# The folded down rows of an FFN taken through DRAM, with other staging places and another order of the first loads

## The reference

```python
# mixer: a decaying scan over the context, projected, averaged over time, added as one row per batch
x = einsum(kv, W_in) + b_in;  s = K*s + xt (scan);  summary = mean(states @ W_out.T + b_out)
y = Z + summary;  return layernorm(y) * gamma + beta
# FFN: a Hadamard transform ahead of up/gate and one ahead of down
x = fwht(x * SU_ug) / SCALE
x_up, x_gate = x @ W_up.T * (...), x @ W_gate.T * (...)
x = fwht(silu(x_gate) * x_up * SU_dp) / SCALE        # over 2048 columns
x = x @ W_down.T * (Wscale_dp * SCALE)
```

## Time and profile before

| | us |
|---|---|
| median of 3 runs (lowest, highest) | 1591.33 (1587.85, 1596.97) |
| the profiled execution | 1594.04 |
| its span | 1592.0 |
| PE busy | 1426.4 (90%) |
| DVE busy | 1015.2 (64%) |
| ACT busy | 508.8 (32%) |
| POOL busy | 385.4 (24%) |

### The profile page before, as it was taken

How to read it: one execution, slowest core, us unless ns; L and a number is a source line. 1 busy time by engine, 2 the same in 40 slices (tenths; PEclk the granted TensorE clock), 3 DMA queues, 4 the chain that set the end, 5 groups by cost and what they waited for, 6 DMA issues and landing times.

```text
span 1592.0 us, 27268 instructions
## 1 busy us (share of the span) xinstructions
PE 1426.4 (90%) x7616; PEld 770.5 (48%) x7617; DVE 1015.2 (64%) x2461; ACT 508.8 (32%) x922; POOL 385.4 (24%) x315
## 2 busy tenths in 40 slices
PE   5569999999999999888988559997989999999797
PEld 3224444444444444444444236654555666666464
DVE  6738866964874555577775546654556666666465
ACT  1324443443343333322222123322222333333232
POOL 1000000000000000034555534342334433444243
PEclk9789999999999999999999779998999999999899
DMA  9664776765675687646747558887888989899787
GB/s 377 167 229 166 248 238 222 240 223 191 210 243 193 216 273 252 224 147 221 256 190 261 197 174 221 226 197 172 207 216 207 236 234 233 219 221 228 165 146 130
DMA packets 133349, 342.82 MB, mean 215 GB/s; under 512 B 15152, under 2 KB 19760, under 8 KB 126896
## 3 DMA queue, kind: packets, MB, share of 16 engines
q1 hardware_dynamic: 74464, 207.51, 39.4%
q0 software_dynamic: 34928, 87.05, 24.2%
q10 hardware_dynamic: 23904, 47.61, 9.7%
HBM read 190.23 MB, written 147.69 MB: 212 GB/s over the span
## 4 chain that ended last, share of the span: by engine, by line
PE 59%; DMA 16%; DVE 8%; issue 7%; SPq 4%; another core or an unknown queue 3%; ACT 3%; ACTq 1%; POOLq 0%; DVEq 0%
PE PS L1394 16%; PE PS L1392 16%; PE PS L1393 16%; DMA rows_by_expert<-X 6%; DMA BIG<-split_experts 4%; PE PS L1620 3%; DMA split_experts<-HT 2%; PE PS L1647 1%; PE PS L1646 1%; SPq L348 1%; DMA BIG<-in_wdT 1%; PE PS L1355 1%; PE PS L1530 1%; PE PS L1635 1%
## 5 line engine op out<-in xcount | busy, mean ns | idle before, releaser
L557 POOL DMA_INDIRECT out<-BIG,EX x160 | 249.1, 1557 | 412.9 <-issue 206.0
L1392 PE MATMUL PS<-BIG 128*128 x804 | 276.0, 343 | 2.8 <-issue 2.0
L1393 PE MATMUL PS<-BIG 128*128 x804 | 275.9, 343 | 0.0
L1394 PE MATMUL PS<-BIG 128*128 x804 | 275.6, 343 | 0.0
L1392 PE MATMUL PS<-HT,BIG 128*128 128x512 f16 (+1 forms) x512 | 195.0, 381 | 7.1 <-ACT EX L607 2.8
L1393 PE MATMUL PS<-HT,BIG 128*128 128x512 f16 (+1 forms) x512 | 194.8, 380 | 0.0
L1394 PE MATMUL PS<-HT,BIG 128*128 128x512 f16 (+1 forms) x512 | 194.6, 380 | 0.0
L535 POOL DMA_INDIRECT rows_by_expert<-HT,POS x128 | 124.3, 971 | 141.7 <-DVE POS L1211 107.6
L1392 PE MATMUL PS<-BIG,EX 128*128 128x512 f16 (+1 forms) x384 | 146.3, 381 | 6.4 <-DVE EX L1153 5.0
L1393 PE MATMUL PS<-BIG,EX 128*128 128x512 f16 (+1 forms) x384 | 146.2, 381 | 0.0
L1394 PE MATMUL PS<-BIG,EX 128*128 128x512 f16 (+1 forms) x384 | 146.0, 380 | 0.0
(11 more groups left out here) (224 smaller groups left out, 2244.1 us busy)
## 6 DMA issues: line engine op xcount, KB each, us to landing
BIG<-rows_by_expert ACTq DMA_DIRECT2D x166, 280.0 KB
HT<-in_experts SPq DMA_DIRECT2D x64, 640.0 KB, 4.6
BIG<-split_experts SPq DMA_DIRECT2D x32, 1152.0 KB
split_experts<-HT SPq DMA_DIRECT2D x96, 320.0 KB, 2.5
CST<-in_kv SPq DMA_DIRECT2D x64, 256.0 KB, 4.5
split_context<-RT SPq DMA_DIRECT2D x64, 256.0 KB, 4.3
BIG<-split_context SPq DMA_DIRECT2D x8, 2048.0 KB
rows_by_expert<-X SPq DMA_DIRECT2D x32, 280.0 KB
```

Of the source, the lines that this page charges most:

```text
L557: pool.indirect_dma_start(a_out, bass.IndirectOffsetOnAxis(ap=IDY[:, u % V:u % V + 1], axis=0), yt[u % V], None, compute_op=ALU.add).then_ ...
L1392: mm(out, lh, rh, start=first, stop=False)
L1393: mm(out, lh, rl, start=False, stop=False)
L1394: return mm(out, ll, rh, start=False, stop=last_group)
```

## The change

Four things change.

1. **wd1 goes through DRAM.** ACT stores four blocks of wd1 (1 MB) at a time to a new DRAM tensor `d_down`, from its own queue, as soon as they are copied. SP waits for all four stores (`s_wst`, 64) and loads chunks 0 to 3, 4 to 7 and later 8 to 15 in three transfers. The sixteen moves are gone.
2. **Other staging places.** Weights chunk 1 is staged at BIG 8192 (inside wd1) and no longer at X 2048, chunk 2 at BIG 10240, and so on. SP loads chunks 0, 1 and 2, POOL the other five. The load of batch 1's x no longer waits for `s_wul` but for `s_w2p` = 4.
3. **Order of the first loads.** The first of the six context loads goes ahead of x, the second between two loads of W_down, one weights chunk ahead of the fourth context load, and the last two context loads behind the router's weights and the first context piece.
4. **Sums of context spread singly.** `sum_context(n)` is now one of twelve sums. Two stand ahead of batch 0's first layer norm, none ahead of `spread(0)`, four between the splits of the transposed tiles, one ahead of each Hadamard split, two behind the last.

```diff
-        wst = [f32(t, o, (KC, 512)) for t, o in ((HT, 0), (X, 2048), (BIG, 8192), (BIG, 10240),
-                                                 (BIG, 12288), (BIG, 14336), (X, 4096), (X, 6144))]
+        wst = [f32(t, o, (KC, 512)) for t, o in ((HT, 0), (BIG, 8192), (BIG, 10240), (BIG, 12288),
+                                                 (BIG, 14336), (X, 4096), (X, 6144), (X, 4096))]
-            def move_chunk(c):
-                sp.dma_start(wd2_chunk(c), wd1[c * 8:(c + 1) * 8, :, :].rearrange("p b d -> p (b d)"))\
-                    .then_inc(s_rel[min(c // 4, 2)], 16)
-
+            def load_chunks(i):
+                first, count = (0, 4, 8)[i], (4, 4, 8)[i]
+                sp.dma_start(wd2[i], d_down.rearrange("(c p) d -> p c d", p=P)[:, first:first + count, :]).then_inc(s_rel[i], 16)
+
+            load_context(0)
             load_x(0, TT)
...
             load_piece(0)
-            sp.wait_ge(s_w1, FC)
-            for c in range(FC):
-                if c == 8:
-                    sp.wait_ge(s_ttr, KC + 8)
-                    for h in range(2):
-                        sp.dma_start(est[h], a_exp[0:1, :, h * EH:(h + 1) * EH].rearrange("a p w -> p (a w)")).then_inc(s_est[h], 16)
-                move_chunk(c)
+            for h in range(4, 6):
+                load_context(h)
+            sp.wait_ge(s_wst, 16 * 4)
+            for i in range(2):
+                load_chunks(i)
+            for c in range(1, 3):
+                load_weights(c)
+            sp.wait_ge(s_ttr, KC + 4)
+            load_chunks(2)
+            sp.wait_ge(s_ttr, KC + 8)
+            for h in range(2):
+                sp.dma_start(est[h], a_exp[0:1, :, h * EH:(h + 1) * EH].rearrange("a p w -> p (a w)")).then_inc(s_est[h], 16)
             sp.wait_ge(s_w2p, 4)
-            load_weights(1)
-            sp.wait_ge(s_wul, 2)
             load_x(TT, 2 * TT)
...
-            pool.wait_ge(s_rel[2], 16 * 8)
-            for c in range(2, 4):
-                load_weights(c)
-            pool.wait_ge(s_wul, 3)
             pool.wait_ge(s_st, 2)
+            load_weights(3)
+            pool.wait_ge(s_sb, 1)
             load_weights(4)
...
             for i in range(FC):
                 down_rows(i)
+                if i % 4 == 3:
+                    act.wait_ge(s_w1, i + 1)
+                    act.dma_start(d_down.rearrange("(p b) d -> p b d", b=FC)[:, i - 3:i + 1, :], wd1[:, i - 3:i + 1, :])\
+                        .then_inc(s_wst, 16)
...
+            for n in range(2):
+                sum_context(n)
             dve.wait_ge(s_x, 16)
             mixer_ln(0, 0)
...
             inverse_root(0)
-            for h in range(2):
-                sum_context(h)
             dve.wait_ge(s_rows, 80)
             spread(0)
...
             for k in range(KC):
+                if k != 2:
+                    sum_context(2 + min(k, 2))
+                else:
+                    ffn_weights_lo(0)
                 chunk_lo(0, k)
-                if k == 1:
-                    ffn_weights_lo(0)
-                if k == 2:
-                    sum_context(2)
+            sum_context(5)
             for c in range(2):
                 down_lo(c, 4 + c)
             for j in range(KC):
+                sum_context(6 + j)
                 hadamard_lo(0, j)
-                if j < 3:
-                    sum_context(3 + j)
+            for n in range(10, 12):
+                sum_context(n)
```

More of the change, by code:

```diff
@@ L272, in build @@
         s_cx0, s_xr2 = sem("first_context_landed"), sem("later_x_landed")
-        s_cx = [sem(f"mixer_context_landed{i}") for i in range(1, B)]
-        s_ws = [sem(f"ffn_weights_landed{i}") for i in range(4)]
+        s_cx = [sem(f"mixer_context_landed{i}") for i in range(5)]
+        s_ws = [sem(f"ffn_weights_landed{i}") for i in range(5)]
         s_wd = [sem(f"down_rows_landed{i}") for i in range(2)]
-        s_rel = [sem(f"down_chunks_moved{i}") for i in range(3)]
+        s_rel = [sem(f"down_chunks_landed{i}") for i in range(3)]
+        s_wst = sem("down_rows_stored")
         s_cpl, s_chi, s_clo, s_cst = (sem(n) for n in (
@@ L356, in _ @@
             sp.dma_start(tri[:, :, :], a_tri).then_inc(s_rows, 16)
-            for h in range(2):
[L358 to L361, removed]
+            load_down(0)
+            load_context(1)
+            load_down(1)
+            sp.wait_ge(s_ttr, KC)
+            for i in range(2, 4):
                 load_down(i)
-            for h in range(2, 4):
-                load_context(h)
+            load_context(2)
             load_weights(0)
-            for h in range(4, 6):
-                load_context(h)
+            load_context(3)
             sp.dma_start(gk[:, :, :], a_gk.rearrange("(k p) e -> p k e", p=P)).then_inc(s_gk, 16)
@@ L508, in load_weights @@
             def load_weights(c):
-                pool.dma_start(wst[c], a_wug[c].rearrange("p (k f) -> p k f", k=KC)).then_inc(s_ws[2 + c % 2], 16)
-            pool.wait_ge(s_rel[2], 16 * 8)
-            for c in range(2, 4):
-                load_weights(c)
-            pool.wait_ge(s_wul, 3)
+                pool.dma_start(wst[c], a_wug[c].rearrange("p (k f) -> p k f", k=KC)).then_inc(s_ws[3 + c % 2], 16)
             pool.wait_ge(s_st, 2)
+            load_weights(3)
+            pool.wait_ge(s_sb, 1)
             load_weights(4)
-            pool.wait_ge(s_wul, 4)
-            pool.wait_ge(s_sb, 1)
-            load_weights(5)
-            for c in range(6, 8):
+            for c in range(5, 8):
                 pool.wait_ge(s_wul, c - 1)
-                pool.wait_ge(s_w2p, (12, 16)[c - 6])
+                pool.wait_ge(s_w2p, (12, 16, 16)[c - 5])
                 load_weights(c)
@@ L580, in ffn_weights_hi @@
             def ffn_weights_hi(c):
-                act.wait_ge(s_ws[c if c < 2 else 2 + c % 2], 16 * max(c // 2, 1))
+                act.wait_ge(s_ws[c if c < 3 else 3 + c % 2], 16 * max((c - 1) // 2, 1))
                 if c == 1:
@@ L997, in ffn_add, with sum_context @@
                     v.tensor_tensor(xt(b * TT + t), xt(b * TT + t), Z[:, t, :], ALU.add).then_inc(s_x2, 1)
-            def sum_context(h):
-                dve.wait_ge(s_cx[h // 2], 32)
-                for i in range(2):
-                    dve.wait_ge(s_ttr, KC + 2 * h + i)
-                    k, b = h % 2 * 2 + i, 1 + h // 2
-                    v.tensor_tensor_reduce(out=cxr[h][:, i, :], in0=cxr[h][:, i, :], in1=vrow[:, ::-1], scale=1.0, scalar=0.0,
-                                           op0=ALU.mult, op1=ALU.add, accum_out=cm[:, k, b:b + 1]).then_inc(s_ttr, 1)
+            def sum_context(n):
+                h, i = n // 2, n % 2
+                dve.wait_ge(s_cx[min(h, 4)], 16 if h < 4 else 32)
+                dve.wait_ge(s_ttr, KC + n)
+                k, b = h % 2 * 2 + i, 1 + h // 2
+                v.tensor_tensor_reduce(out=cxr[h][:, i, :], in0=cxr[h][:, i, :], in1=vrow[:, ::-1], scale=1.0, scalar=0.0,
+                                       op0=ALU.mult, op1=ALU.add, accum_out=cm[:, k, b:b + 1]).then_inc(s_ttr, 1)
             def states(first, last, bank):
@@ L1437, in _ @@
             pe.wait_ge(s_w1, FC)
-            pe.wait_ge(s_rel[0], 16 * 4)
+            pe.wait_ge(s_rel[0], 16)
             for c in range(2):
```

13 lines of the change are left out of this document (7 added, 6 removed).

## The result

| | before | after |
|---|---|---|
| median of 4 runs (lowest, highest), us | 1592.36 (1587.85, 1596.97) | 1573.81 (1572.69, 1584.23) |
| the profiled execution, us | 1594.04 | 1573.78 |
| its span, us | 1592.0 | 1571.7 |
| up_gate(0) starts, us | 82.30 | 75.72 |
| PE resumes behind the wait for the spread, us | 117.57 | 101.96 |

The ratio of the medians is 0.9893 with a 95% interval of 0.9853 to 0.9933: the kernel became faster by 1.1%. The forecast was 1577 (1570 to 1588).

The account below looks back on a forecast made before the run. PE bounds the kernel from 126 us on, so gains lie in four earlier PE waits. 12.5 us at PE's resumption (3.2 from Hadamard steps) plus 1.5 for the clock gave 14.0: 1594.0 to 1580.0 profiled, median 1577.3, range 1570 to 1588.

Parts of the forecast that it names:

- Start of DVE: Before the first chunks: `spread(0)` at 29.0 instead of 31.55, 2.5 us won, hidden behind the chunks' arrival.
- The round trip: wd1 through DRAM: bytes done at 59, plus 0.7 completion and 6.6 load, so first chunks at 66.
- the lower end (63.5): Also the lower case: stores served ahead of loads, leaving 2.5 us of bytes and some 2 us latency behind 59.
- The round trip by itself wins nothing for the first chunks: First chunks through DRAM come at 66, where the moves already had them (65.98).
- Hadamard steps: Between first chunks (landing at T) and up_gate(0): single sums bring up_gate(0) at T + 13.1, not T + 16.3; 3.2 us won.
- The spread: PE's wait for a summary's spread: 2.2 us instead of 11.5, resuming at 105.1 not 117.57; 12.5 us won in all.
- The clock: PE's products after the spread wait: less time at the low clock, 0 to 3.3 us won, taken as 1.5.
- The sum: Whole kernel: 12.5 + 1.5 = 14.0 us less, profiled execution 1580.0, median 1577.3.
- The late round trip: Rival: first chunks only at 70 to 76, gain 4 to 10 us, time 1581 to 1587; chance 0.17.
- the slower case: Rival: stores at the moves' rate, chunks at 80 to 115; at T = 90 the time is 1601; chance 0.06.
- Given back in the FFN: Rival: from 126 us on the expert halves' chain sets the pace, PE waits for DVE; 1588 to 1592; chance 0.08.
- The case "more": Rival: first chunks (T) near 63.5 and clock never low, 18 us and beyond won, 1570 to 1573; chance 0.10.

Follow-up runs that it names:

- experiment 5: Kernel before with only the DRAM round trip (four stores, three loads) replacing the moves; places, load order and sums as before: 1587.98 us, ratio to before 0.9980.
- experiment 6: Changed kernel with ACT's four stores issued together behind the sixteenth block: 1579.95 us, ratio to the kernel before 0.9924.
- experiment 8: Changed kernel with the last two context loads issued behind the load of chunks 0 to 3: 1538.96 us, ratio to the kernel before 0.9886.
- experiment 2: Kernel before with only the context sums spread singly over the Hadamard steps: 1559.38 us, ratio to before 1.0005.
- Experiment 4: Changed kernel with the context sums back in pairs behind the first three Hadamard splits: 1545.21 us, ratio to the kernel before 0.9935.
- experiments 3: Changed kernel with the sixteen moves inside SBUF instead of the DRAM round trip, weights chunk 1 waiting for them: 1560.06 us, ratio to the kernel before 1.0017.
- experiment 1: Kernel before with DVE's three spreads of f = 1 moved ahead of context_lo(1): 1548.03 us, ratio to before 0.9949.
- The repeat: Changed kernel run again unchanged, on another chip: 1540.63 us, ratio to the kernel before on that chip 0.9877.
- experiments 6 and 10: 10: changed kernel with last two context loads behind chunks 0 to 3 and spreads moved to f = 0: 1534.88 us, ratio to before 0.9861.

## Why the prediction was right

Direction, mechanism and size held; two terms were mis-sized, in opposite directions.

- **Start of DVE.** Predicted `spread(0)` at 29.0 and the transposes at 53.2; measured 28.84 and 53.03. As forecast, it hid behind the chunks.
- **The round trip, "59 + 0.7 + 6.6 gives 66".** This is the term that was mis-sized. The chunks came at 63.05, just under the lower end (63.5). All my bytes had to be moved by 59 because the DMA engines are full; they were full (422 GB/s), but the stores need not be last among these bytes. They were complete at 54.4. With the old order of loads they are complete at 59.0 (experiment 5), and where they are last the chunks come at 66.05 (experiment 6). Part of it went back in the second leg: 8.5 us and not 6.6, since the load stood behind two context loads (experiment 8: 5.5). That 63.05 lies so near to 63.5 is partly luck: the lower case did have the stores ahead of the loads, but as 4.5 us behind 59, and it came as 8.5 us behind 54.4. With the 2.9 us earlier chunks everything behind moved by 2.9.
- **"The round trip by itself wins nothing for the first chunks."** Nearly: experiment 5 has them 1.4 us earlier than the kernel before, and 0.4 earlier than experiment 2, which has the moves.
- **Hadamard steps.** Predicted T + 13.1, measured 63.05 + 12.67; won 3.65 us and not 3.2. Experiment 4 has the same size (3.3) by undoing it.
- **The spread.** Predicted: the copy of the summaries at 98.35, 6.7 us to the first spread, a wait of 2.2. Measured 94.98, 6.9 (the spread's row at 101.22 and its 0.7) and 2.42. The difference of 3.4 is the chunks' 2.9 and the Hadamard steps' 0.45. The piece was issued at 87.08 and was split by ACT from 91.87; DVE came to it at 99.85 with 7 us to spare. With experiments 3 and 5 the cause is shown too: the round trip has to change together with the places and waits, or SP's chain stands.
- **The clock, +1.5.** It came as 0. PE resumes with rows of 2.07 and 3.78 us, the same as in the earlier trace rows, and a granted clock of 0.52 for 6.8 us. A wait of 2.4 us had cost as much as one of 11.5. It need not: in experiment 6, after 2.42 us too, the first row took 1.38 us (the next 3.78), and experiment 1, after 1.03 us, has 1.12 and 3.50.
- **The sum.** 12.5 + 1.5 = 14.0 predicted; 2.9 more from the chunks, 0.45 more from the steps, 0.2 less from a wait of 2.4, and the clock's 1.5 left out make 15.7; 15.6 was measured at the resumption. The profiled execution came out 6.2 us under 1580.0: 1.6 of these are in the start, the others in later stages. The median came out 3.5 under 1577.3.
- **Rivals.** The late round trip and the slower case fall: no engine waited for chunks after 63.05, and the rate was 422 and 399 GB/s beside reads. "Given back in the FFN" falls by the 15.5 us that are left at its end. The case "more" named the two terms rightly: T near 63.5 came, the clock didn't. No part that was run by itself does it: single sums are worth at most 1.4 us, the way through DRAM 3.6, and places, order of loads and sums without DRAM less than nothing; together they give 15.5. The order of the first loads and the new places were not run each by itself.

What stays open: why the profiled pair is 20.3 us apart at the end and 15.5 at the end of the FFN. The ratio's interval (11 to 23 us) holds both. The repeat leads by 15.0 in the FFN as well; nothing in the changed lines reaches the later stages. Open too is how much of 1 to 3 us in the kernels with moves is the trace's own: with no edit that reaches it, weights chunk 1 came 2.5 us earlier in experiment 1 than in the kernel before, of which there is one trace.

## What to carry to other kernels

Look at which wait ends last, and ask of each edit whether it moves that end: single sums gave at most 1.4 us ahead of a fixed release and 3.3 once the release was free to move. A spread, or any short step that PE waits for, should not stand in an engine's program behind a split whose data is a transfer late; moving the spreads ahead of it took 7.5 to 10 us. When bytes are added to DMA engines that are full, count not only when all bytes are done but which of them must be: issued early they take their share from loads that nobody waits for, and the load that reads them back should not be queued behind such loads. And before a small difference between two traces is given to an edit, look whether something that the edit can't reach moved by as much.

## What the runs showed of the hardware

- Transposing rows by moves out of 8 partitions goes at 60 GB/s; 4.19 MB took some 58 us in experiment 3, 72 GB/s on average. The same bytes stored to DRAM from 128 partitions and loaded back ran at 399 to 422 GB/s in all, with other loads beside them, and the first chunks were back 17 us after the last store was issued.
- Rates of 422 GB/s held while reads and writes were mixed, as in stretches of reads alone (418). The sum of the prediction by the limit of about 358 GB/s in the Trainium skill (SBUF — State Buffer, section "A bandwidth-pool intuition that's wrong") doesn't fit this trace for writes either; one core was running.
- Low stretches of the clock come, go and grow with small shifts in order. Experiment 4 has one more than the changed kernel (0.53 for 3.4 us, behind a wait of 2.62 us), which cost 1.7 us; the kernel before has none behind its wait of 2.40 us. The changed kernel has one of 3.4 us from 84.7 on, though PE's rows show no wait since 75.7: it comes behind the summaries' products (L1353, 3.6 us). In experiments 6 and 10 the stretch there is 6.8 us long and costs some 1 to 2 us more. At this size of effect a gain read from rows at one clock is uncertain by that much.
